# A four-layer graph network on one core: the setup is split, the first and last layers are rewritten, and layer 1's mark products are put together ahead of the scores

## The reference

```python
q, k, v = x @ Wq.T, x @ Wk.T, x @ Wv.T                       # layer 0
wei = softmax(where(adj == 0, -inf, q @ k.T * scale)) + adj
x = layernorm(x + wei @ v)
e = leaky_relu(g_r[:, :, None] + g_l[:, None]) . w_attn      # layer 1, 8 heads
x = layernorm(x + leaky_relu(softmax(masked e) @ g_r))
h = relu(hi[:, :, None] + hj[:, None] + b1)                  # layer 2
x = layernorm(x + sum_j adj * (_layernorm(h @ W2 + b2) * gamma + beta))
a = adj + eye; d = rowsum(a) ** -0.5                         # layer 3
x = layernorm(x + (a * d[:, :, None] * d[:, None, :]) @ (x @ weight) + bias)
```

## Time and profile before

| what | us |
|---|---|
| median of 3 runs (1572.91 to 1576.82) | 1573.96 |
| the profiled execution, its own time | 1573.45 |
| its span | 1571.7 |
| setup, to the first instruction of layer 0 | 24.9 |
| layer 0, to its last instruction | 139.9 |
| layer 1, from its first instruction at 174.5 to the table load at 965.0 | 790.5 |
| layer 2, from 967.8 to its last instruction at 1446.1 | 478.3 |
| the end, from there to the end of the span | 125.6 |

### The profile page before, as it was taken

How to read it: one execution, slowest core, us unless ns; L and a number is a source line. 1 busy time by engine, 2 the same in 40 slices (tenths; PEclk the granted TensorE clock), 3 DMA queues, 4 the chain that set the end, 5 groups by cost and what they waited for, 6 DMA issues and landing times. The chain is left out here.

```text
span 1571.7 us, 28366 instructions
## 1 busy us (share of the span) xinstructions
PE 1380.7 (88%) x9081; PEld 1163.2 (74%) x9081; DVE 1251.6 (80%) x2450; ACT 1044.8 (66%) x2743; POOL 55.9 (4%) x88
## 2 busy tenths in 40 slices
PE   3666588999999999999999986999999999995764
PEld 2555366688888888888888885888888888884654
DVE  4888478778787878878787644898889989987888
ACT  2565588766666666666666213888888888886554
POOL 1000000000000000000000000010010110100000
PEclk9998699999999999999999997999999999998877
DMA  2220266888887878878888665988787788771122
GB/s 75 68 67 27 112 258 247 320 310 292 299 304 291 308 288 308 306 283 309 299 296 303 236 243 206 349 274 279 271 271 280 267 275 278 268 253 47 45 74 67
DMA packets 137585, 367.61 MB, mean 234 GB/s; under 512 B 12896, under 2 KB 71904, under 8 KB 137440
## 3 DMA queue, kind: packets, MB, share of 16 engines
q1 hardware_dynamic: 137040, 365.81, 65.8%
q10 hardware_dynamic: 400, 0.00, 0.0%
HBM read 231.54 MB, written 134.22 MB: 233 GB/s over the span
## 5 line engine op out<-in xcount | busy, mean ns | idle before, releaser
L874 DVE TENSOR_TENSOR b_wt<-bank,b_aT 128x512 f32<-128x512 f32 (+1 forms) x192 | 109.7, 599 | 95.2 <-PE bank L688 88.1
L647 PE MATMUL wide<-b_vv,put_w 128*128 128x512 f32 (+1 forms) x384 | 170.9, 527 | 12.8 <-DVE b_vv L823 10.8
L1054 PE MATMUL wide<-W2c,c_h 128*128 128x128 f32 x1280 | 173.9, 275 | 0.0
L1054 PEld LDWEIGHTS wide<-W2c,c_h 128*128 128x128 f32 x1280 | 170.4, 193 | 3.3
L664 PE MATMUL bank<-b_wt,b_SITl 128*128 128x136 f32 x1280 | 160.1, 280 | 9.4 <-DVE b_wt L874 9.4
L664 PEld LDWEIGHTS bank<-b_wt,b_SITl 128*128 128x128 f32 x1280 | 156.3, 190 | 16.0 <-DVE b_wt L874 12.0
L823 DVE TENSOR_TENSOR b_vv<-duo,b_vv 128x512 f32<-128x512 f32 (+1 forms) x192 | 113.8, 600 | 51.4 <-ACT b_vv L744 51.4
L688 PE MATMUL bank<-b_grl,b_SJl 128*128 128x128 f32 x1280 | 153.4, 275 | 0.6 <-ACT b_aT L751 0.6
L688 PEld LDWEIGHTS bank<-b_grl,b_SJl 128*128 128x128 f32 x1280 | 148.7, 192 | 2.8 <-issue 2.6
L1184 DVE TENSOR_REDUCE c_var<-c_ysq 128x4 f32<-128x512 f32 (+1 forms) x192 | 113.5, 591 | 43.2 <-ACT c_ysq L1113 43.0
L648 PE MATMUL wide<-b_SI,put_m 128*128 128x512 f32 (+1 forms) x192 | 131.6, 686 | 0.0
(11 more groups left out here) (212 smaller groups left out, 3180.4 us busy)
## 6 DMA issues: line engine op xcount, KB each, us to landing
si_d<-b_SI SPq DMA_DIRECT2D x64, 640.0 KB, 2.9
sj_d<-b_SJ SPq DMA_DIRECT2D x64, 640.0 KB, 4.1
sit_d<-b_SIT SPq DMA_DIRECT2D x64, 640.0 KB, 5.3
b_SJl<-sj_d SPq DMA_DIRECT2D x64, 640.0 KB, 5.8
b_SITl<-sit_d SPq DMA_DIRECT2D x64, 640.0 KB, 5.9
c_SJ<-sj_d SPq DMA_DIRECT2D x64, 640.0 KB, 5.3
c_SI<-si_d SPq DMA_DIRECT2D x64, 640.0 KB, 6.6
c_SIT<-sit_d SPq DMA_DIRECT2D x64, 640.0 KB, 4.2
```

Source lines behind the costliest of these rows:

```text
L647: pe.matmul(out, e.put_w[:, pos, :], vv[:, (pos + k) % 2, 0:width(k)], start=(pos == 0), stop=False)
L874: v.tensor_tensor(wt[:, mb, 4 * k:4 * k + rr, 0:P].rearrange("p r (h f) -> p r h f", h=HEADS), ring[k][:, 0:P * rr].rearrange("p (r h f) - ...
L1054: d = pe.matmul(bY[k][:, a:a + P], h[:, k, a:a + P], e.W2c[:, :], start=False, stop=(j == last))
```

## The change

1. **Setup** keeps the loads of Wq, Wk, Wv and the first four groups, `M`, `WvT`, the identity and a new matrix `cen` (identity minus 1/128). `WvT` becomes the product of Wv's transpose with `cen`. Everything else moves into layer 0: 19 DMAs to SP's queue ahead of its reloads, the masks and constants to POOL, two transposes to PE (at group 4), the means of W2, b2, weight and bias to DVE (at n = 13 and 14). The weight and the bias of layer 3 are now centred.
2. **Layer 0** is written out with no loop, one stage deeper. The mask is made in bf16 and added to the scores by a product with the identity (L220 of the new file); the sum x plus output, and its centring, come from a product of x's transpose with `cen` into the same bank (L239); entries that are neither 0 nor 1 are counted by a product with ones (L252). DVE copies the result to `cur` (L340); ACT squares a group in one instruction and DVE sums the squares (L343).
3. **Layer 1**: the three mark products stand together ahead of the first score.
4. **Layer 3** is written out with no loop, and the `roots` block ahead of it is gone. The degrees of layer 0 serve for all 64 graphs at once. POOL makes diag(d) (`dga`) and the scaled `cur` (`xd`), 8 instructions of 128x128 a group (L1758, L1766). PE multiplies adj by `dga`; DVE adds `dga` on the way out of PSUM (L1848). The bias comes from a product of ones with `b3x` (L1777), DVE adds the scaled `cur` in 4 instructions (L1856) and scales the result (L1862).

```diff
@@ layer0
+                sp: 2 x raw, 8 x wcol, W1s (2), W2c, W3, b1c, b2r, gam, bet, bir -> late_in
+                for f in range(4, NG):
+                    sp.wait_ge(xT_mm, f - 3)
+                    sp.dma_start(xin[:, f % 4, :, :], e.x_v[:, G * f:G * f + G, :]).then_inc(x_in[f % 4], 16)
+                    sp.wait_ge(pr_ok, f - 3)
+                    sp.wait_ge(deg_ok, f - 3)
+                    sp.dma_start(ain[:, f % 4, :, :], e.adj_v[:, G * f:G * f + G, :]).then_inc(x_in[f % 4], 16)
...
+                for n in range(-3, NG):
+                    f, h, p = n + 3, n + 2, n + 1
...
+                        pe.wait_ge(drop_ok, h + 1)
+                        if h > 0:
+                            pe.wait_ge(ex_ok, G * h)
+                        pe.matmul(bS[:, :], e.identb[:, :], drop[:, h % 2, :, :], start=True, stop=False)
+                        pe.wait_ge(t_ok, h + 1)
+                        for g in range(G):
+                            m = pe.matmul(bS[:, P * g:P * g + P], tT[:, h % 2, g, :], xT[:, h % 4, g, :],
+                                          start=False, stop=(g == G - 1))
...
+                        for g in range(G):
+                            pe.matmul(bO[:, P * g:P * g + P], xT[:, n % 4, g, :], e.cen[:, :], start=True, stop=False)
+                            m = pe.matmul(bO[:, P * g:P * g + P], prT[:, n % 2, g, :], xv[:, n % 4, g, :], start=False, stop=True)
...
+                        pe.matmul(bD[:, :], e.ones3[:, :], odd[:, f % 2, :, :], start=(f == 0),
+                                  stop=(f == NG - 1)).then_inc(od_mm, 1)
...
-                        q.add(v.tensor_tensor(sm[:, hb, :, :], grp(bS), drop[:, :, :], ALU.add))
-                        v.tensor_reduce(top[:, hb, :], sm[:, hb, :, :], AX.X, ALU.max, negate=True).then_inc(top_ok, 1)
+                        v.tensor_reduce(top[:, h % 2, :], grp(bS), AX.X, ALU.max, negate=True).then_inc(top_ok, 1)
-                        q.add(v.tensor_reduce(e.deg[:, 1, bass.ds(h * G, G)], odd[:, :, :], AX.X, ALU.add))
-                        v.tensor_tensor(res[:, :, :], grp(bO), xin[:, pos % 4, :, :], ALU.add).then_inc(res_ok, 1)
-                        r.add(v.tensor_reduce(mean[:, :], res[:, :, :], AX.X, ALU.add))
-                        r.add(v.tensor_scalar(mean[:, :], mean[:, :], 1.0 / P, None, ALU.mult))
-                        v.tensor_tensor(cur[:, bass.ds(n * G, G), :], res[:, :, :],
-                                        mean[:, :].unsqueeze(2).broadcast_to([P, G, P]), ALU.subtract).then_inc(cen_ok, 1)
+                        v.tensor_copy(cur[:, G * n:G * n + G, :], grp(bO)).then_inc(cur_ok, 1)
+                        v.tensor_reduce(e.sqsum[:, G * l:G * l + G], sq[:, l % 2, :, :], AX.X, ALU.add).then_inc(sum_ok, 1)
@@ prepare
-                q.add(v.tensor_reduce(worst[:, 1:2], bank[:, P + B:P + 2 * B], AX.X, ALU.max))
+                q.add(v.tensor_reduce(worst[:, 1:2], e.banks[6][:, :], AX.X, ALU.max))
@@ layer1_packed
-                        pe.matmul(out, e.put_w[:, pos, :], vv[:, (pos + k) % 2, 0:width(k)], start=(pos == 0), stop=False)
-                        pe.matmul(out, e.put_m[:, pos, :], s.SI[:, pos % 4, chunk(k)], start=False,
+                        pe.matmul(out, e.put_w[:, pos, :], vv[:, (pos + k) % 2, 0:width(k)], start=False,
                                   stop=(pos == R - 1)).then_inc(e_mm, 1)
+                    def mark_rows():
+                        if pos == 0 and n > 0:
+                            pe.wait_ge(es_ok, K)
+                        for k in range(CHUNKS):
+                            pe.matmul(bE[:, chunk(k)], e.put_m[:, pos, :], s.SI[:, pos % 4, chunk(k)], start=(pos == 0), stop=False)
@@ layer3
+            @block.gpsimd
+            def _(pool):
+                for n in range(NG):
...
+                    for g in range(G):
+                        i = G * n + g
+                        t = pool.tensor_scalar(dga[:, n % 4, g, :], ident[:, :], inv[:, i:i + 1], 1.0, ALU.mult, ALU.mult)
...
+                        t = pool.tensor_scalar(xd[:, n % 4, g, :], cur[:, i, :], both[:, i:i + 1], 1.0, ALU.mult, ALU.mult)
...
-                            pe.matmul(bG[:, P * g:P * g + P], xd[:, b, g, :], aT[:, b, g, :], start=True, stop=False)
-                            m = pe.matmul(bG[:, P * g:P * g + P], xd[:, b, g, :], ident[:, :], start=False, stop=True)
+                            m = pe.matmul(bG[h % 2][:, P * g:P * g + P], xd[:, h % 4, g, :], aT[:, h % 2, g, :], start=True, stop=True)
...
+                        v.tensor_tensor(aT[:, f % 2, :, :], grp(bA[f % 2]), dga[:, f % 4, :, :], ALU.add).then_inc(aT_ok, 1)
...
+                            v.scalar_tensor_tensor(res[:, n % 2, g, :], cur[:, i, :], e.rstd[:, i:i + 1],
+                                                   bO[n % 2][:, P * g:P * g + P], ALU.mult, ALU.add).then_inc(res_ok, 1)
...
+                        v.tensor_tensor(cur[:, G * l:G * l + G, :], res[:, l % 2, :, :],
+                                        scale[:, l % 2, :].unsqueeze(2).broadcast_to([P, G, P]), ALU.mult).then_inc(scaled, 1)
```

More of the change, by code:

```diff
@@ L121, in _ @@
             def _(sp):
[L123 to L127, removed]
+                for k in range(2):
+                    sp.dma_start(raw[:, k, :], (w.W_l, w.W_r)[k]).then_inc(late_in, 16)
+                for h in range(HEADS):
+                    sp.dma_start(e.wcol[HF * h:HF * (h + 1), :],
+                                 w.w_attn.rearrange("(f a) -> f a", a=1)).then_inc(late_in, 16)
@@ L129, in _ @@
             @block.tensor
             def _(pe):
[L131 to L144, removed]
+                for n in range(-3, NG):
+                    f, h, p = n + 3, n + 2, n + 1
+                    if has(f):
+                        pe.wait_ge(x_in[f % 4], 32 * (f // 4) + 32)
+                        if f > 0:
@@ L164, in step @@
                         m.then_inc(xv_mm, 1)
[L165 to L173 removed]
+                        pe.wait_ge(odd_ok, f + 1)
@@ new lines, in flat @@
+                def flat(k, matrix, mean, out):
+                    v.wait_ge(late_in, NL)
+                    s.add(v.tensor_reduce(rmean[:, k:k + 1], matrix, AX.X, ALU.add))
+                    s.wait()
+                    s.add(v.tensor_scalar(rmean[:, k:k + 1], rmean[:, k:k + 1], -1.0 / P, None, ALU.mult))
+                    s.wait()
+                    return v.tensor_scalar(out, matrix, rmean[:, k:k + 1], None, ALU.add)
+                for n in range(-3, NG + 2):
+                    f, h, p, l = n + 3, n + 2, n + 1, n - 2
+                    if has(p):
+                        v.wait_ge(ex_ok, G * (p + 1))
+                        if p >= 2:
+                            v.wait_ge(prT_mm, p - 1)
+                        v.reciprocal(rden[:, :], den[:, p % 2, :]).then_inc(rden_ok, 1)
+                        v.wait_ge(rden_ok, p + 1)
@@ L1655, in _, with load @@
-                for n in range(NG - 4, NG):
-                    store(n)
-                sp.wait_ge(stored, 16 * NG)
+                def load(n):
+                    sp.dma_start(ain[:, n % 4, :, :], e.adj_v[:, G * n:G * n + G, :]).then_inc(a_in[n % 4], 16)
+                for n in range(4):
+                    load(n)
+                for n in range(-3, NG + 2):
+                    if has(n + 7):
+                        sp.wait_ge(aT_mm, n + 4)
+                        load(n + 7)
+                    if has(n - 1):
+                        sp.wait_ge(scaled, n)
+                        sp.dma_start(e.out_v[:, G * (n - 1):G * n, :], cur[:, G * (n - 1):G * n, :]).then_inc(stored, 16)
@@ L1659, in _ @@
             @block.tensor
             def _(pe):
-                def step(K, pos, inner):
-                    n = 4 * K + pos
-                    f, h = n + 2, n + 1
-                    if group(n, inner):
+                for n in range(-3, NG):
+                    f, h = n + 3, n + 1
+                    if has(n):
                         pe.wait_ge(g_ok, n + 1)
-                        if inner or n > 0:
-                            pe.wait_ge(out_read, n)
+                        if n >= 2:
+                            pe.wait_ge(res_ok, G * (n - 1))
+                        pe.matmul(bO[n % 2][:, :], e.ones3[:, :], e.b3x[:, :], start=True, stop=False)
@@ L1722, in step @@
[L1722 to L1729 removed]
+                        act.copy(gT[:, h % 2, :, :], grp(bG[h % 2])).then_inc(g_ok, 1)
@@ L2052, in adjacency_stack @@
         e.M = M
+        e.cen = cen
         e.WvT = WvT
```

614 lines of the change are left out of this document (294 added, 320 removed).

## The result

The changed kernel takes **1467.35 us** (median of 4 runs, 1466.42 to 1467.57), the kernel before 1573.81 beside it (1572.91 to 1576.82). The ratio is 0.9313, 95% interval 0.9301 to 0.9324: 106.5 us less. I had forecast 1487, with a range from 1470 to 1515. The direction was right.

The account below looks back on a forecast made before the run. It took the bound to differ by stage: DVE in layer 0 and the end, PE in mid layer 1, DVE's constants in setup. -52.4 + 0.5 - 6.4 - 28.4 = -86.7 from 1573.45 gave 1487 us, range 1470 to 1515.

Parts of the forecast that it names:

- POOL's price: Layer 3: 128 POOL instructions at 0.59 us each, 75.5 us; called most open, from 0.50 (-11 us) to 0.80 (+27 us).
- the rival had 0.75 to 1.0 us: Layer 3: two-operation POOL instructions cost 0.75 to 1.0 us, adding 20 to 52 us, 1507 to 1539; chance 0.13.
- POOL's pauses beside DVE: Layer 3: POOL stands still beside one DVE instruction a group, L1862; 12 x 0.6 = 7.2 us.
- POOL sets the pace: Layer 3: POOL bounds each group at about 5.2 us, against 6.9 of DVE's before; span change -28.4 us.
- Setup: Before layer 0: with fewer loads ahead, SP's issues end at 8.2 and layer 0 begins at 8.7 us.
- POOL's first instruction late: Setup and ahead of dga: POOL's first instruction of a kind starts 5.2 us late, up to 1493; chance 0.04.
- Layer 0's pace and bound: Layer 0: PE, no longer DVE, sets the pace at 5.87 us a group, 13 groups making 76.3 us.
- tail: End of layer 0: 8.0 us from the last scores to the last output product, then 2.3 more, 10.3 in all.
- PE's clock falls in layer 0: Layer 0: a third of PE's products at the lower level bring back 25 us, 1512; chance 0.08.
- Between the layers: Between layers 0 and 1: `prepare` reduces 512 columns where it reduced 64, +0.5 us.
- Layer 1's early steps: Layer 1, first 14 steps: two marks leave the path while PE waits, 14 x 0.46 = -6.4 us.
- Layer 1's late steps: Layer 1 from step 14: same columns, no waits, so 0, with 0.1 us a step, 5 us, allowed both ways.

Follow-up runs that it names:

- e1: Changed kernel with POOL's multiplication forms swapped: layer 3's dga and xd with one operation, layer 2's bb with two; 1493.31 us against 1467.35.
- e7: Changed kernel with layer 3's dga and xd made on DVE, 512 columns an instruction, and POOL's loop taken out; 1469.91 us against 1467.35.
- e8: Changed kernel with 14 unused PE products added behind layer 2's last product and 7 ahead of layer 3's first; 1467.49 us against 1467.35.
- e10: Changed kernel with layer 3's dga and xd of groups 0 and 1 made on DVE, POOL beginning at group 2; 1463.72 us against 1467.35.
- e6: Changed kernel without layer 0's products of x with cen, so without its residual; 1454.74 us against 1467.35.
- e11: Changed kernel with layer 0's four means on DVE moved one each to groups 5, 7, 9 and 11; 1462.05 us against 1467.35.
- e5: Changed kernel with layer 0's means on DVE moved in pairs from groups 13 and 14 to groups 6 and 8; 1464.08 us against 1467.35.
- e2: Changed kernel with layer 1's marks put back behind each score, as before the change; 1467.18 us against 1467.35.
- e4: Changed kernel with layer 1's marks behind the second gather from step 15 on, save in each eighth step; 1470.43 us against 1467.35.
- e9: Changed kernel with layer 1's third mark back behind the third score in all steps, the first two together ahead of the scores; 1461.44 us against 1467.35.

## Why the prediction was wrong by 20 us

- **POOL's price** (the step "128 x 0.59 = 75.5") is the term that failed. The row that I took, L1025, is of one operation, and I treated the second operation as something that can only cost: the rival had 0.75 to 1.0 us, and the lower bound of 0.50 was a guess. It measured 0.37, and e1 turned it into 0.60 and back by the form alone. That is 26.5 us. "A multiplication by 1 makes no difference or costs" was an assumption that no row carried.
- **POOL's pauses beside DVE** (12 x 0.6 = 7.2 us) were of the right kind, though fewer us: in the changed kernel a group of POOL's takes 3.2 us beside L1862 and 2.77 without, which makes 49.9 - 16 x 2.77 = 5.6 us in all; in e1, at the forecast's price, they were 2.7, and that and the instructions' pace of 0.579 for 0.59 are the other 5.9 us of layer 3. The Trainium skill (SBUF — State Buffer, Who interferes with whom) says that a DVE instruction with two SBUF inputs contends with a GpSimd instruction that reads SBUF; L1862 is such an instruction and the trace agrees: the four POOL instructions at 1418.18 take 0.5 us longer, and L1862 beside them takes 0.89 us, where it takes 0.69 in e7, in which POOL has no work.
- **"POOL sets the pace"** held for the end of layer 3, with 1.9 us to the first instruction and 12.7 behind the last. It did not hold for the first eight groups: with POOL at 0.37 they come at PE's 2.89 us, and POOL's 3.2 counts only from about 1438 on. That POOL sets layer 3's end is shown by e8 (a faster PE changes nothing) and e10 (a shorter POOL does).
- **Setup** held: 7.8 for 8.7. SP's last two issues took 1.04 and 0.90 us, as part of the forecast had it.
- **POOL's first instruction late** (the rival at 0.04): no. The first mask came 0.23 us after the fills and the first dga 0.1 after `inv` was ready. The Trainium skill (GPSIMD Engine Reference, Instruction dispatch) has about 6 us for a freshly loaded kernel; no such gap stands in this trace.
- **Layer 0's pace and bound** held: 5.72 us for 5.87, PE without a wait, and e6 shows that it is PE that paces. The fill was 15.5 us for 17.0. The **tail** failed: 17.2 us behind the last scores for the 10.3 forecast. Two assumptions were wrong together: that means at n = 13 and 14 lie beside other work when the last group has no other work beside it, and that PE comes back from a wait of 4.7 us at full speed. In e11, with neither in it, the tail is 13.1 us, so these two were 4.1 of the 6.9. The other 2.8 stays in e11: the last output waits 0.9 us there for L340 to copy the one before, which the forecast did not have, and the rest is not taken apart. Of the 6.9, and the 3.0 between the layers, e11 won back 5.3 net. The rival "PE's clock falls in layer 0" came true in that tail alone, as the granted clock shows (0.97 over the layer).
- **Between the layers** I had 0.5. POOL's row of the bias ends 2.3 us behind the rest. I had named that chain, with "up to 3 us", and taken it at nothing; e5 and e11, in which the next block starts 0.3 us behind DVE, show it.
- **Layer 1's early steps** held: 0.52 us each for 0.46. One, right behind a wait of 1.9 us of PE for ACT, ran at a granted clock of 0.50 from 201.4 to 204.8 and lost 1.6 us (9.02 us, 7.42 in e5). It did so in e2 too, with the old order, and not in the kernel before, nor in e4, e5, e6 or e11, which have the same wait and the changed order of the marks there. So it isn't the marks' doing; what decides it stays open.
- **Layer 1's late steps** were put at 0 with 5 us to either side. They cost 0.115 us each, 5.6 us, just past what I allowed; it is also the sign of being wrong that I had named (the 550 us stretch changing by more than 5 us), as 47 such steps lie in it. The reason that I gave (the same columns to stream, so the same time) was wrong: the third mark stood where PE had room for it, and e9 shows that place.
- **The sums.** The terms of layer 0's group add up to 5.90, where I went on with 5.87: 0.4 us over 13 groups. My lower bound of 1470 is 1469 by its own terms, and the upper one of 1505 has none: POOL at 0.80, the price that I named, would have made it 1514. None of this decides: the measured time lies below all of them.

## What to carry to other kernels

Before costing an instruction by a row of another form, ask whether the form itself could be cheaper, not only dearer: a second operation that changes nothing took 38% off POOL's multiplication here. And look at the pieces even when the total is nearly right: here 34 us one way stood against 14 the other. Work that moves off a busy engine "beside" the others needs a place with something beside it; the last two groups of a loop are not one, and a few such instructions on DVE and POOL cost 5 us. And where PE is never idle, a product may still be free in one place and not in another: compare the pieces of one step in both orders, since the sum of columns does not tell.

## What the runs showed of the hardware

- POOL's multiplication of a 128x128 fp32 tile in SBUF by a scalar per partition: 0.60 us with one operation, 0.37 with two, in two layers and on different data (e1).
- PE's granted clock around pauses: 0.50 from 1392.6, 1.4 us ahead of a pause of 10.6 us, to 1413; in e8, with 28 and 14 records of added products in that pause, 1.00 from 1396.6 to 1406.7, and then again 0.50 from 1406.8 to 1410.1. In layer 0 a wait of 4.7 us for the last weights was followed by products at the lower level; one of 2.6 was not in e11, and in e5 it was, 0.7 us later.
- A DVE instruction of 512 fp32 columns costs less in a full queue than its duration says: in e7 a group has 4.27 us of DVE's durations (four of 0.685, four of 0.34, one of 0.17) and one came every 3.65 us. Neighbours overlap at their ends, so a sum of durations overstates a pace that DVE sets. POOL's overlap too, 0.35 us from start to start for 0.37.
